# Another accumulator for one block, an earlier weight split and one more whole group at the start of a feature-interaction kernel

## The reference, cut to what matters

```python
h = x
for i in range(3):
    out = relu(einsum('bfd,bgd,fgs->bsd', x, h, W[i]) + b[i][None, :, None])
    if i != 2:
        h, direct = out[:, :64], out[:, 64:]
    else:
        direct = out
    outs.append(direct)
return sum(concatenate(outs, axis=1), axis=-1)     # (512, 256)
```

## Time and profile before

| | |
|---|---|
| median of three runs | 571.18 us |
| the profiled execution | 570.96 us |
| its span (first to last instruction) | 569.1 us, so 1.9 us lie around it |
| PE busy | 558.0 us (98%) |
| DVE busy | 531.8 us (93%) |
| POOL busy | 505.5 us (89%) |
| ACT busy | 365.8 us (64%) |
| mean granted TensorE clock | 0.996 |
| chain that ended last | PE 88%, POOL 5%, issue 3% |

### The profile page before, as it was taken

The page is one execution under the profiler, slowest core; times in us unless marked ns, Lnnn a source line. Parts: engine busy times, 40 slices in busy tenths (PEclk is TensorE's granted clock), DMA queues, the critical chain, the costliest instruction groups (busy, mean ns, idle before and its releaser), DMA issues.

```text
span 569.1 us, 7814 instructions
## 1 busy us (share of the span) xinstructions
PE 558.0 (98%) x2003; PEld 377.6 (66%) x2003; DVE 531.8 (93%) x516; ACT 365.8 (64%) x409; POOL 505.5 (89%) x222
## 2 busy tenths in 40 slices
PE   8899999999999999999999999999999999999997
PEld 4354666767676666667767667676767766666765
DVE  5679999999999999999999999999999999999975
ACT  1255775766767576676776758586676757668562
POOL 1257999899999999999899999989999999999995
PEclk9899999999999999999999999999999999999999
DMA  8998935738375582846649285573837558262001
GB/s 331 412 413 329 383 115 181 299 124 332 101 261 225 179 332 85 311 157 203 276 146 346 68 295 214 166 313 113 329 111 256 229 173 337 79 210 80 0 2 37
DMA packets 27390, 121.68 MB, mean 214 GB/s; under 512 B 3312, under 2 KB 3440, under 8 KB 25328
## 3 DMA queue, kind: packets, MB, share of 16 engines
q1 hardware_dynamic: 27376, 121.52, 58.8%
HBM read 120.98 MB, written 0.52 MB: 213 GB/s over the span
## 4 chain that ended last, share of the span: by engine, by line
PE 88%; POOL 5%; issue 3%; DMA 1%; DVE 1%; ACT 1%; SPq 0%; POOLq 0%; DVEq 0%; ACTq 0%
PE acc L572 88%; POOL z_lo L294 4%; DMA xfirst<-x 1%; POOL w_lo L540 1%; DVE z_whole L431 0%; DVE z_raw L431 0%; ACT h L660 0%; ACT last L660 0%; ACT z_hi L657 0%; SPq L304 0%; SPq L327 0%; DVE z_hi L292 0%; ACT direct L660 0%; DVE sums L454 0%; DVE z_lo L291 0%
## 5 line engine op out<-in xcount | busy, mean ns | idle before, releaser
L294 POOL TENSOR_TENSOR z_lo<-z_raw,z_hi 128x1024 fp32r<-128x1024 f32 x202 | 477.8, 2406 | 25.2 <-ACT z_hi L657 22.7
L657 ACT CAST z_hi<-z_raw 128x1024 fp32r<-128x1024 f32 (+1 forms) x215 | 216.9, 1022 | 111.5 <-DVE z_raw L431 94.0
L431 DVE TENSOR_TENSOR z_raw<-h,xwide 128x1024 f32<-128x1024 f32 x189 | 225.6, 1214 | 4.7 <-ACT h L660 3.0
L572 PE MATMUL acc<-z_hi,w_hi 128*128 128x512 f32 (+1 forms) x543 | 210.1, 460 | 0.8 <-ACT last L660 0.8
L572 PE MATMUL acc<-z_hi,w_lo 128*128 128x512 f32 x530 | 171.7, 395 | 0.0
L572 PE MATMUL acc<-z_lo,w_hi 128*128 128x512 f32 x498 | 160.0, 397 | 2.3 <-POOL z_lo L294 1.9
L572 PEld LDWEIGHTS acc<-z_hi,w_hi 128*128 128x128 f32 (+1 forms) x543 | 102.2, 188 | 60.6 <-issue 39.5
L572 PE MATMUL acc<-z_whole,w_whole 128*128 128x512 f32 x256 | 120.0, 592 | 0.0
L572 PEld LDWEIGHTS acc<-z_hi,w_lo 128*128 128x128 f32 x530 | 99.4, 188 | 24.0
L572 PEld LDWEIGHTS acc<-z_lo,w_hi 128*128 128x128 f32 x498 | 92.6, 187 | 28.4 <-POOL z_lo L294 5.8
L431 DVE TENSOR_TENSOR z_whole<-h,xwide 128x1024 f32<-128x1024 f32 x68 | 82.3, 1213 | 6.2 <-PE acc L572 3.9
(11 more groups left out here) (25 smaller groups left out, 155.1 us busy)
## 6 DMA issues: line engine op xcount, KB each, us to landing
xwide<-x SPq DMA_DIRECT2D x160, 512.0 KB, 4.7
xfirst<-x SPq DMA_DIRECT2D x13, 2048.0 KB, 7.8
xfirst<-x SPq DMA_DIRECT2D x4, 768.0 KB, 12.2
xwide<-w SPq DMA_DIRECT2D x2, 1024.0 KB, 16.7
xwide<-x SPq DMA_DIRECT2D x1, 1280.0 KB, 11.8
xfirst<-x SPq DMA_DIRECT2D x2, 512.0 KB, 11.4
xwide<-x SPq DMA_DIRECT2D x1, 768.0 KB, 9.2
z_raw<-w0b SPq DMA_DIRECT2D x1, 640.0 KB, 6.0
```

What stands on the lines that cost most here:

```text
L294: return eng.tensor_tensor(lo[0:rows, 0:n, :], z[0:rows, 0:n, :], hi[0:rows, 0:n, :].bitcast(F32), ALU.subtract)
L431: nc.vector.tensor_tensor(dst, in0, in1, ALU.mult).then_inc(made[kind], 1)
L572: return nc.tensor.matmul(dst, w[0:rows, place, :], z[0:rows, t - G * g, :], start=first and first_g and t == G * g, stop=final and t == T ...
L657: nc.scalar.copy(z_hi[0:rows, slot("PV", pair, par, pos, HI_RING), 0:n, :], src).then_inc(hi_made, 1)
```

## The change

Four edits, all at the start of the program; the loop over the later steps is as before.

- Layer 0 of block 1 (in step 0) accumulates in `acc[2]` instead of `acc[0]`, and `relu0(0)` reads it there. PE so doesn't wait for `acc_read[0]` in step 0. Layer 2's first group in step 1, which writes `acc[2]` next, waits for `acc_read[0]` at 2 instead.
- ACT copies the factor for step 1 (`copy_xrep(1)`) before `relu0(0)`.
- ACT and POOL split layer 2's weights at entry 0 of step 1, and ACT does so before `relu1(1)`. The load of `w2` is issued one place earlier, ahead of head 1 of block 2.
- In step 0 group 14 is W instead of P, and 15 comes before 17 (and its `xwide` load too).

```diff
-ORDER_0 = "00W 01W 02W 03W 11W 13W 10W 12W 16W 14P 17W 15P 18P 19V"
+ORDER_0 = "00W 01W 02W 03W 11W 13W 10W 12W 16W 14W 15P 17W 18P 19V"
-SPLIT2_AT_1 = 2
+SPLIT2_AT_1 = 0
@@ SP @@
             load_first(2, xfirst_head_in[0], range(0, 1 + G))
+            sp.dma_start(stage[2][:, 0:SPLIT_COUNT[2], :], w2).then_inc(w_staged[2], 16)
             load_first(2, xfirst_head_in[1], range(1 + G, 1 + 2 * G))
-            sp.dma_start(stage[2][:, 0:SPLIT_COUNT[2], :], w2).then_inc(w_staged[2], 16)
@@ PE, contract @@
-                dst = acc[layer][:, :]
+                dst = acc[2 if isinstance(j, int) and (layer, j) == (0, 0) else layer][:, :]
                 if first_g:
-                    ready(pe, acc_read[layer], j + (1, 0, -1)[layer])
+                    if isinstance(j, int) and (layer, j) == (2, 1):
+                        pe.wait_ge(acc_read[0], 2)
+                    if isinstance(j, int) and layer == 0 and j < 2:
+                        ready(pe, acc_read[0], j)
+                    else:
+                        ready(pe, acc_read[layer], j + (1, 0, -1)[layer])
@@ ACT, relu0 and step @@
-                a = acc[0]
+                a = acc[2 if isinstance(j, int) and j == 0 else 0]
                     if pos == RELU0_AT and has(1, BLOCKS - 2):
                         relu0(j, par)
+                    if isinstance(j, int) and j == 1 and pos == SPLIT2_AT_1:
+                        split_layer(2)
                     if pos == RELU1_AT and has(1, BLOCKS):
                         relu1(j, par)
                     if pos == RELU2_AT and has(2, BLOCKS):
                         relu2(j)
-                    if isinstance(j, int) and j == 1 and pos == SPLIT2_AT_1:
-                        split_layer(2)
                 if isinstance(j, int) and j == 0:
+                    copy_xrep(1)
                     relu0(j, par)
-                    copy_xrep(1)
```

## The result

| | before | after |
|---|---|---|
| median of 8 executions | 571.12 us | 568.52 us |
| lowest to highest | 569.45 to 573.93 | 568.47 to 568.69 |
| profiled execution | 570.96 | 568.55 |
| its span | 569.1 | 566.3 |

The ratio is 0.995, 95% interval 0.9932 to 0.9968. The changed kernel takes 2.6 us less, and 0.2 more than the 568.3 that were forecast. Two things were not forecast: the changed kernel varies by 0.2 us where the old one varies by 4.5, and in the profiled executions the span fell by 2.8 but the time by only 2.4.

A forecast was written before the change was run, and what follows sets the result against it. PE runs without a wait from 90.77, a moment set by when POOL's row at 50.21 starts. That start, through loads, ACT and DVE, comes 2.9 earlier: 570.96 - 2.9 = 568.1, median 568.3 us; own range 567.7 to 568.9, with rivals 567.3 to 569.8.

The forecast's parts named there:

- PE in step 0: Without the bank wait at 15.57, PE reaches 22.2 instead of 25.84 and ends step 0 at 38.6, 3.0 earlier.
- The 0.2 us of stop that were to stay: PE's wait after 00W ends at 17.3, since 01W's products cannot be there before 17.5.
- the 3.6 us: PE in step 0: first `w_whole` matmul at 22.2 in place of 25.84, from losing the stop and half clock.
- ACT in front of step 1: ACT is later than PE: weight cast at 37.7, `relu1` 39.6 for 41.82, DVE's first layer-2 product 40.95, 2.2 earlier.
- POOL in step 1, and the hold: POOL's first group starts at 47.3 instead of 50.21; the 2.9 us lead holds to PE's last wait, 87.9 for 90.77.
- the 1.9 us around the span: Time of the profiled execution outside its 569.1 span, kept unchanged in forecasting 568.1, and 568.3 for the median.
- The clock's fall: Rival: PE's clock falls all the same, costing PE 1.7 in step 0; lead 2.2, time 569.0; chance 0.11.
- PE's own gain: Rival: PE's gain in step 0, 3.9 less 0.3 for 14W, reaches the end: 567.6; chance 0.07.
- The lock: Rival: DVE's first layer-2 product is held 3.25 until POOL's weight subtraction ends at 44.2: 571.5; chance 0.04.
- The late weights: Rival: each us `w2` lands behind 37.7 moves the whole ring by one; landing at 42.0 gives 572.6; chance 0.04.
- The chances between "faster" and "same": Whole kernel at the 0.5% bound (2.86 us, 568.3): faster 0.48, same 0.48, slower 0.04.

The follow-up runs named there:

- The kernel with the late weights: Changed kernel with `w2`'s load issued last of block 2's pieces, landing at 40.3 instead of 37.2: 571.12 us, ratio 1.0009 to the kernel before.
- the filler: Kernel before with 8 added matmuls of zeros into acc1 in PE's stop of 2.19 us at 15.57: 569.29 us, ratio 0.9971.
- The run with two small operations: Changed kernel plus one small ACT copy and one small POOL subtraction (128x8) in idle time before 24 us: 568.42 us, ratio 0.9965.

## Why the prediction was right, and where it was not

**PE in step 0.** Right to 0.1 us: first `w_whole` matmul at 22.24 (22.2), end of step 0 at 38.68 (38.6). The 0.2 us of stop that were to stay are not listed as idle time in PE's rows. But the 3.6 us rest on one execution in which the clock fell. Against the one at full clock, 24.21 - 22.24 = 2.0 us are what the bank gives there.

**ACT in front of step 1.** Right: weight cast 37.72 (37.7), `relu1` 39.65 (39.6), DVE 41.01 (40.95). That ACT and not PE is latest there was argued then and is shown now. With 17W first PE was through 0.4 us later, and with 14P 0.3, and the span did not change. With the cast taken out of the way `relu1` did wait for PE.

**POOL in step 1, and the hold.** Right: 47.38 (47.3), and PE's last wait 87.90 (87.9). The kernel with the late weights shows the same chain with a later start, and POOL's first group came there within 0.1 us of what was expected (50.00 for 49.9).

**The value of the parts.** The prediction costed the change as a whole and left open which part carries it. The runs: the bank alone 568.52, all else alone nothing in the time, the whole 568.52. That the first and the last are equal is a sum and no sign that the rest does nothing: ACT's order and the load bring 0.5 us once the bank is there (568.03), and 14W loses 0.5. The cast ahead of `relu1` cleared POOL's way by as much as it delayed `h1`; inside `relu1` it brings 0.6. And of the 2.87 us at PE's last wait, 90.77 - 89.15 = 1.62 came with the fall of the clock in the profiled execution, and 1.25 are left at full clock. In the median span at full clock the bank alone brings 0.8 us (567.5 to 566.7) and the rest 0.4 (to 566.3).

**The mis-sized term.** "570.96 - 2.9 = 568.1, and for the median 568.3": the 1.9 us around the span were carried over as they stood. They became 2.25, and no run shows why. Of the forecast 2.9, 2.87 came at PE's last wait, 2.4 at the profiled execution's end. The other half of the same sentence, the median of before, is that of a mixture: by the table above most often a time of the second row, and next often one of the first. Against the profiled execution without a fall (569.33) the change gains 0.8 us, against those with a mean clock of 0.991 (574.0) 5.5. So the time after, 568.5, was forecast by a mechanism that the runs bear out, but that the gain in the medians came near 2.9 is luck in part: it hangs on the profiled execution before and the median before having come from the same row.

**The rivals.** The clock's fall did not come in any of the eight executions after (mean clock 0.999 or 1.000). In all nine kernels with the bank moved and the weights on time it came once in 81 executions, and that once it cost 0.3 us (568.80 with the bank alone), not the 0.7 of the rival's sum. PE's own gain did not reach the end: at full clock 2.0 us earlier at the first `w_whole` matmul became 1.25 at PE's last wait. The lock did not show: the products beside POOL's weight subtraction (41.01 and 43.28) kept their length. The late weights had the right price and did not occur. The chances between "faster" and "same" at 0.5% were near even, and the ratio, 0.995, fell on the line.

## What to carry to other kernels

A median may be a mixture: look at the clock and the time of each execution before a difference of half a per cent is given a cause. A short stop of PE can cost more than its length, where the clock falls with it. Filling it with useless matmuls made this kernel steadier, and a spare accumulator made it steadier and 0.8 us faster. In a chain where two engines are within a microsecond, ask which is latest at each joint: edits to the other are worth little until the first has moved, and an instruction put ahead of a critical one in an engine's list can give back what it brings. When two variants take the same time, compare the span and the time around it too: equal times were twice the sum of a gain and a loss here.

## What the runs showed of the hardware

- The fall of the clock differs between executions with the same stop. With a stop of 2.19 us the clock stayed at 1.00, was 0.50 for 3.41 us from 18.35 (PE went on at 17.75), or was 0.50 for 6.83 us from 16.86 (PE went on at 17.64; 6.05 of them busy), in three executions. In two kernels, the bank alone and the filler, the profiled execution had 0.50 at about 12.1 to 15.5, behind stops of 2.02 and 1.90 us in step -1 (block 0's layer 0); in the changed kernel a stop of 1.81 us there was followed by no fall.
- A half-clock stretch can cost nothing at the end. With the weights late, the profiled execution had 0.50 from 46.27 to 49.68, behind a stop of 2.78 us in step 1; the executions with a mean clock of 0.996 or 0.997 and those with 1.000 took the same 571.0 to 571.3 us, and PE's last wait, at 90.55, was for POOL.

```profile
46.27:49.68 3.41, 3.41 (x5) 1.35 (x4) 3.41 (x5) 0.80 (x1) 0.56 (x1) 0.50 1.02 404
```

- The time outside the span depends on the program. It was 2.2 to 2.3 us in the seven kernels with 14W and nothing added to ACT and POOL, 1.7 to 1.9 in those with 14P, though the work behind the last matmul is the same. The profile's queue of instruction loads (line: queue, packets, MB, share) differs too, first with 14W and then with 14P:

```profile
q14 instruction: 7, 0.06, 0.0%
```

```profile
q14 instruction: 8, 0.07, 0.0%
```

The run with two small operations has 7 packets as well and 1.9 us outside, so the packets don't explain it, and the cause stays open.
